# A third chain, in two halves of tiles, for a layer's second feed-forward in a two-layer fused kernel

## The reference, cut to what matters

```python
h = layernorm(x) * ln1_g + ln1_b
src2 = diff_attn(h) @ Wo.T + bo          # 16 x 16 heads inside a row, rmsnorm of each head's output
conn = x + src2
h2 = layernorm(conn) * ln2_g + ln2_b
y = conn + relu(h2 @ W1.T + b1) @ W2.T + b2   # 256 -> 1024 -> 256
x = x + y
x = x + product_key_ffn(layernorm(x))    # sim = n5 @ cmat (1024 scores a row), top 16 of 64 twice,
                                         # top 16 of their 50 sums, softmax, gelu(n5 @ wd50) @ wu50
```

## Time and profile before

| | us |
|---|---|
| median of 3 runs (lowest, highest) | 3261.49 (3259.35, 3266.36) |
| the profiled execution's own time | 3247.05 |
| its span, first to last instruction | 3245.3 |
| first group's front alone | 0 to 290 |
| seven joint groups | 290 to 2934, 376 to 379 each |
| last group's back alone | 2934 to 3245.3 |

### The profile page before, as it was taken

The page is one execution under the profiler, slowest core; times in us unless marked ns, Lnnn a source line. Parts: engine busy times, 40 slices in busy tenths (PEclk is TensorE's granted clock), DMA queues, the critical chain, the costliest instruction groups (busy, mean ns, idle before and its releaser), DMA issues. The chain is left out here.

```text
span 3245.3 us, 47685 instructions
## 1 busy us (share of the span) xinstructions
PE 2507.4 (77%) x16384; PEld 1810.7 (56%) x16384; DVE 1848.2 (57%) x7166; ACT 879.3 (27%) x1914; POOL 875.3 (27%) x1076
## 2 busy tenths in 40 slices
PE   5796898768885889848987699858999489876544
PEld 3585567545763558635675457635586356753422
DVE  2313456755648548574557556485485645673557
ACT  1212242223422233222421234222332224212210
POOL 0002114222233223241143223332232411432042
PEclk8698999979997999979998789978999699986666
DMA  6085145141533326241451416333261314512100
GB/s 234 13 281 200 66 127 205 65 148 40 194 137 112 140 78 225 76 141 64 134 197 66 148 46 203 120 125 127 81 227 70 139 66 128 203 66 108 27 0 7
DMA packets 215066, 392.39 MB, mean 121 GB/s; under 512 B 83728, under 2 KB 167952, under 8 KB 189616
## 3 DMA queue, kind: packets, MB, share of 16 engines
...
HBM read 350.55 MB, written 38.67 MB: 120 GB/s over the span
## 5 line engine op out<-in xcount | busy, mean ns | idle before, releaser
L869 PE MATMUL ps<-xbT,stream 128*128 128x128 f32 x2560 | 316.8, 278 | 11.1 <-DMA stream<-in_experts 6.6
L869 PEld LDWEIGHTS ps<-xbT,stream 128*128 128x128 f32 x2560 | 303.4, 193 | 29.6 <-DMA stream<-in_experts 14.4
L301 POOL TENSOR_TENSOR hTB<-pb,sbuf 128x2048 f32<-128x2048 f32 x32 | 152.3, 4772 | 394.8 <-DVE pb L1829 394.8
L529 POOL TENSOR_TENSOR rstdB<-veB,mhalf 128x3 f32<-128x3 f32 (+1 forms) x112 | 81.2, 725 | 589.3 <-DVE veB L1433 562.4
L481 POOL TENSOR_TENSOR rstdA<-veA,mhalf 128x4 f32<-128x4 f32 x24 | 24.5, 1019 | 634.0 <-DVE veA L1404 634.0
L882 PE MATMUL ps<-stream,hTA 128*128 128x256 f32 x640 | 152.5, 381 | 18.0 <-DVE hTA L1662 12.2
L1112 PE MATMUL ps<-ident,work 128*50 128x128 f32 x32 | 12.0, 375 | 194.9 <-POOL work L643 194.9
L869 PE MATMUL ps<-xbT,ctxA 128*128 128x128 f32 x1280 | 157.8, 277 | 2.5 <-DMA ctxA<-in_experts 2.5
L869 PEld LDWEIGHTS ps<-xbT,ctxA 128*128 128x128 f32 x1280 | 150.8, 192 | 12.0 <-DMA ctxA<-in_experts 6.5
L680 PE MATMUL ps<-cmat,aTB 128*128 128x512 f32 x256 | 123.6, 628 | 20.9 <-DVE sbuf L1918 10.7
L1766 DVE TENSOR_TENSOR xB<-ps,xB 128x256 f32<-128x256 f32 x32 | 13.6, 425 | 218.2 <-PE ps L1007 217.3
...
## 6 DMA issues: line engine op xcount, KB each, us to landing
...
```

The costliest lines, as they stand in the source:

```text
L301: return e.tensor_tensor(out.rearrange("p (a d h) -> p a d h", a=8, d=16), a.unsqueeze(2).broadcast_to([P, 8, 16, 16]), vals[:, t, :].rear ...
L529: nc.gpsimd.tensor_tensor(rstdB[:, span(tag, p)], veB[:, span(tag, p)], mhalf[:, 0:len(PARTS[tag][p])], ALU.pow).then_inc(pool_done, O.ste ...
L869: ins = mm(ps[:, 2 * (b % 2) + u, f * P:(f + 1) * P], wu[:, u, k, f * P:(f + 1) * P], xbT[:, b % 2, k, :], start=k == 0, stop=k == KT - 1)
```

## The change

1. ORDER gets a third letter, "s", for a **side** chain. It takes the norm `h2`, the feed-forward, the norm `n5` and the product `h50` with `wd50` out of the back chain (15 slots fewer: 103) and does them in two halves of two tiles: 10 slots for each half and one for `h50`. The new ORDER has 192 letters.
2. A half has its own PSUM bank (6 for half 0, 7 for half 1) and its own 2048 columns for the ReLU's output (`hF2`, in `work`). An `f1` product is now 256 columns wide, its two outputs share the bank's halves, and each pair of outputs waits for the ReLU of the pair before.
3. In the new ORDER half 0 starts behind value slot 3.c and ends ahead of selection slot 0.0: `h2` around block 9, `f1` and `f2` with block 10 and value slots 4.a to 5.c between them, then the gate of 11. Half 1's norm `h2` comes just ahead of selection 0.0, its `f1` between selection 0.0 and 0.2 with the up product of 11, its `f2` and `n5` behind selection 1.1, with the up product of 12, then `h50`. The up product of block 14 again stands between selection 2.1 and 2.2; as many instructions of VectorE follow it as before.
4. `l4 o` moves from VectorE to GpSimd, right behind the power, and works in place in `ob`; the values' sums go to `ob` in SBUF and no longer to PSUM bank 6; `prod` has one buffer, `rep64` moves to `hTB`.
5. The relay has a semaphore for each tile: the write of tile 1 is issued ahead of the read of tile 0, those of 2 and 3 around the read of tile 1, and the expert blocks' row loads come behind all of them.
6. ORDER also changes earlier: some front slots of the first 40 stand one or two places elsewhere, the third slot of the shared expert's end stands ahead of `v`, and the first gate product stands behind two score slots, no longer ahead of them.

```diff
 ORDER = (
-    "bbbfbbbfbbfbfbfbfbffbfbffbfbfbffbfbfbbfbbffbfbffbffbfbbfbfbffbfbbbbfbffbfbbbbffbbffbbbffbbfbbffb"
-    "fbbfffbbfbffbbffbfbfbbfbbfbbbbbbbbbbbbbbbbbbbfbfbbbbbfbbbfbfbfbfffbfbbbbbbbbbbbbbbbbfbbbbb"
+    "bbbfbbfbbfbfbbfbfbfbfbbfffbffbfbfbfbfbfbbffbfbffbffbfbbfbfbffbfbbbfbbbffbbfbbbffbbffbfbfbbbbbfbf"
+    "ffbfbfbffbbbffbfbfsfsbfbsfssbbssbssbfsssbsbsfssbbbbfbbsssfssbbfbbbffbfffbbbfbbbbbbbbbbbbbbbfbbbb"
 )
...
-        prod = work[:, 0:4096].rearrange("p (s n) -> p s n", s=2)
+        prod = work[:, 0:2048]
...
-        raw = ps[:, 6, :].rearrange("p (s n) -> p s n", s=2)
+        hF2 = work[:, 2048:4096].rearrange("p (f n) -> p f n", f=FF // P)
...
-        rep64 = sbuf[:, 0:1024].rearrange("p (a k) -> p a k", a=NPH)
+        rep64 = hTB[:, 2048:3072].rearrange("p (a k) -> p a k", a=NPH)
...
-        PARTS = dict.fromkeys(("y1", "y2", "h2", "n5"), (range(T - 1), range(T - 1, T)))
-        PARTS.update(dict.fromkeys(("y3", "z", "h1"), (range(HALF), range(HALF, T))))
-
-        TURNED = dict.fromkeys(("y1", "y2", "h1", "h2"), ((5, 0), (6, 0)) * 2)
-        TURNED["n5"] = ((6, 0), (7, 0)) * 2
+        PARTS = dict.fromkeys(("y1", "y2"), (range(T - 1), range(T - 1, T)))
+        PARTS.update(dict.fromkeys(("y3", "z", "h1", "h2", "n5"), (range(HALF), range(HALF, T))))
+
+        TURNED = dict.fromkeys(("y1", "y2", "h1"), ((5, 0), (6, 0)) * 2)
...
-                        def relay(t):
+                        def relay_out(t):
                             sp.wait_ge(act_done, A["qk", t])
                             sp.dma_start(qk[:, t * P:(t + 1) * P, :].rearrange("c n d -> n c d"),
-                                         qk_rows[:, t, :].rearrange("p (c d) -> p c d", c=2)).then_inc(qk_out, 16)
-                            sp.wait_ge(qk_out, 16 * (t + 1))
+                                         qk_rows[:, t, :].rearrange("p (c d) -> p c d", c=2)).then_inc(qk_out[t], 16)
+
+                        def relay_in(t):
+                            sp.wait_ge(qk_out[t], 16)
                             for c, cols, landed in ((1, k_cols, k_in[t]), (0, sbuf[:, 0:1024], q_in)):
                                 sp.dma_start(cols[:, t * D:(t + 1) * D].rearrange("p (n a) -> p n a", n=8),
                                              qk[c, t * P:(t + 1) * P, :].rearrange("(n i) (d a) -> (i d) n a", i=16, d=8)).then_inc(landed, 16)
                         yield
-                        for t in range(T):
-                            relay(t)
-                            yield
-                        for _ in range(9 + 2 + (T + 2) * 3 + 1 + 8 + T + 1 + 1):
+                        relay_out(0)
+                        relay_out(1)
+                        yield
+                        relay_in(0)
+                        yield
+                        relay_out(2)
+                        relay_in(1)
+                        relay_out(3)
+                        yield
+                        relay_in(2)
+                        relay_in(3)
...
+                                pool.wait_ge(pool_done, O["rms", i - 1])
+                                o3 = ob[:, i - 1, :].rearrange("p (a d) -> p a d", a=16)
+                                nc.gpsimd.tensor_tensor(o3, o3, b16(mx[:, (i - 1) % 2, 0:16], 16), ALU.mult).then_inc(
+                                    pool_done, O.step("l4", "o", i - 1))
...
+                    def side():
+                        for p in range(2):
+                            rstd("h2", p)
+                            yield
+                            for t in PARTS["h2"][p]:
+                                wait_scaled(pool, "h2", t)
+                                add("cb", t, xnB[:, t], xnB[:, t], w["b2a"])
+                            for t in PARTS["h2"][p]:
+                                pool.wait_ge(pool_done, O["cb", t])
+                                add("xc", t, xB[:, t], xB[:, t], xnB[:, t])
+                            yield
+                            for _ in range(4 + 2):
+                                yield
+                            rstd("n5", p)
+                            yield
+                            yield
...
+                    def side():
+                        for p in range(2):
+                            bank, tt, cols = 6 + p, PARTS["h2"][p], slice(p * 2 * P, (p + 1) * 2 * P)
+                            yield
+                            for t in tt:
+                                turn("h2", t, hh, TURNED["h2"][t])
+                            yield
+                            for f in range(FF // P):
+                                if f == 0:
+                                    pe.wait_ge(act_done, A["h2", "T", tt[1]])
+                                elif f % 2 == 0:
+                                    pe.wait_ge(act_done, A["h2", "relu", p, f - 1])
+                                for k in range(KT):
+                                    ins = mm(ps[:, bank, f % 2 * 2 * P:(f % 2 + 1) * 2 * P], kt("w1a")[:, k, f * P:(f + 1) * P],
+                                             aTB[:, k, cols], start=k == 0, stop=k == KT - 1)
+                                ins.then_inc(pe_done, PE.step("h2", "f1", p, f))
+                                if f % 2:
+                                    yield
+                            w2v = w["w2a"].rearrange("p (f d) -> p f d", f=FF // P)
+                            pe.wait_ge(act_done, A["h2", "relu", p, FF // P - 1])
+                            for t in tt:
+                                for f in range(FF // P):
+                                    ins = mm(ps[:, bank, t % 2 * D:(t % 2 + 1) * D], hF2[:, f, t % 2 * P:(t % 2 + 1) * P], w2v[:, f, :],
+                                             start=f == 0, stop=f == FF // P - 1)
+                                ins.then_inc(pe_done, PE.step("h2", "f2", t))
+                                yield
+                            yield
+                            for t in tt:
+                                turn("n5", t, xnB, TURNED["n5"][t])
+                            yield
+                        pe.wait_ge(act_done, A["n5", "T", T - 1])
+                        for t in range(T):
+                            ins = project(ps[:, 7, t * NP:(t + 1) * NP], aTB, t, kt("wd50"), slice(0, NP))
+                        ins.then_inc(pe_done, PE.step("h50"))
+                        yield
+
...
+                    def side():
+                        for p in range(2):
+                            yield
+                            turned("h2", p, ("v", T - 1), ("lg2", "lb2"))
+                            yield
+                            for f in range(FF // P):
+                                if f % 2 == 0:
+                                    act.wait_ge(pe_done, PE["h2", "f1", p, f + 1])
+                                sa(hF2[:, f, :], ps[:, 6 + p, f % 2 * 2 * P:(f % 2 + 1) * 2 * P], ACT.Relu, bias=w["b1a"][:, f:f + 1]).then_inc(
+                                    act_done, A.step("h2", "relu", p, f))
+                                if f % 2:
+                                    yield
+                            yield
+                            yield
+                            yield
...
-                            if i >= 2:
-                                t = i - 2
-                                v.wait_ge(pool_done, O["rms", t])
-                                v.wait_ge(vec_done, V["pred", t, 1])
-                                vv.tensor_tensor(ob[:, t, :].rearrange("p (a d) -> p a d", a=16),
-                                                 raw[:, t % 2, :].rearrange("p (a d) -> p a d", a=16),
-                                                 b16(mx[:, t % 2, 0:16], 16), ALU.mult).then_inc(vec_done, V.step("l4", "o", t))
...
+                    def side():
+                        for p in range(2):
+                            variance("h2", p)
+                            yield
+                            scaled_part("h2", p, xnB, hh)
+                            yield
+                            for _ in range(4 + 2):
+                                yield
+                            for t in PARTS["n5"][p]:
+                                v.wait_ge(pe_done, PE["h2", "f2", PARTS["n5"][p][-1]])
+                                v.wait_ge(pool_done, O["xc", t])
+                                vv.tensor_tensor(xB[:, t, :], ps[:, 6 + p, t % 2 * D:(t % 2 + 1) * D], xB[:, t, :], ALU.add).then_inc(
+                                    vec_done, V.step("h2", "f2", t))
+                                stats("n5", xB, smallB, t)
+                            variance("n5", p)
+                            yield
+                            scaled_part("n5", p, xB, xnB)
+                            yield
...
-            group(g, "fb")
-        group(G, "b")
+            group(g, "fbs")
+        group(G, "bs")
```

120 lines of the change are left out of this document (38 added, 82 removed).

## The result

The changed kernel takes 3243.3 us in the median (3236.5 to 3247.6); beside it, in the same rounds, the kernel before took 3261.5 us (3249.3 to 3266.4). The ratio is 0.9952, with a 95% interval of 0.9934 to 0.9970: 10 to 22 us faster. On a second chip it was 0.9959 (0.9940 to 0.9978). The forecast was 3216.5 us, 45 us faster. The direction was right and the time lies in the stated range, but the gain was forecast two and a half times too large.

The account below looks back on a forecast made before the run. No single engine: a joint group was TensorE's work up to block 14, then VectorE's tail. Seven joint groups at -4.3 (-30) and -15 for the last took 3247.05 to 3202, median forecast 3216.5 us, range 3168 to 3264.

Parts of the forecast that it names:

- the earlier edits of ORDER (first 40 slots): Front of each group: slots swap places with the same work, no sure wait gained or lost; 0, bounds -1.5 and +1.5.
- The tail "keeps its length": Joint group from `hid` of block 14 to the selection's end, nearly all VectorE's own work: stays 38.2 us.
- `hid` 14: VectorE's `hid` of block 14 started 2.7 us after its up product; it would now wait for the product: -2.7 us.
- Relay and start of the scores: Joint group: earlier relay write lets the scores start sooner and `combine` end earlier; -1.6 us, bounds 0 and -3.0.
- `f1` in half widths: Joint group's feed-forward: 64 records of 256 columns take 14.0 us against 17.4; -3.0 us, bounds -3.4 and 0.
- old and new waits: TensorE from `combine` to block 14: old waits of 8.9 us go, new ones of 11.9 come, bounds 8.9 and 16.
- Slower: Rival: TensorE's in-order queue held at the ReLU waits; at 1.3 us longer each, +64, 3326 us; chance 0.11.
- nothing: Rival: new waits are 16 us and the clock falls in a half; within 0.2%, 3266 us; chance 0.09.
- better filling: Rival: new waits stay at or below 8.9 us and front slots gain; -76 to -104, about 3170 us; chance 0.24.
- `l4 o` on GpSimd: Joint group's value stage: moving this multiply off VectorE costs nothing, 0; if its cover is gone, 2.9 us a group.
- The last group: Without expert blocks the side chain truly overlaps: relay -4.0, earlier selection -11.3; -15 us, bounds -20 and -4.
- the rival of a low clock through all of half 0: Last group: half 0's products take 13.4 us more and eat the 11.3 gained; 3228 us; chance 0.14.

Follow-up runs that it names:

- e3: The kernel before with only the first 30 letters of ORDER taken from the changed kernel: 3270.3 us, ratio 1.0060 to the kernel before.
- e1: The changed kernel with the first 30 letters of ORDER as in the kernel before: 3224.0 us, ratio 0.9922 to the kernel before.
- e14: e1 run again beside the changed kernel on one chip: 21 us faster than the changed kernel in these rounds.
- e4: The kernel before with only the new relay, ORDER unchanged: 3244.9 us, ratio 0.9982 to the kernel before.
- e6: The changed kernel with the first 30 letters of ORDER as before and the relay in series again: 3229.0 us, ratio 0.9925 to the kernel before.
- e7: e1 with the output scaling `l4 o` back on VectorE, in place in SBUF: 3331.9 us, ratio 1.0232 to the kernel before.
- e13: The changed kernel run again, unedited, on the same chip as e14: 21 us slower than the old front in these rounds.
- e5: The changed kernel with only the first 14 letters of ORDER as before: 3240.7 us, ratio 0.9943 to the kernel before.
- e9: The changed kernel with layer 0's output projection done twice for tiles 2 and 3: 3234.4 us, ratio 0.9954 to the kernel before.

## Why the prediction was right and wrong, point by point

**The step that failed: "the earlier edits of ORDER (first 40 slots) exchange slots with the same work: 0", bounds -1.5 and +1.5 for a group.** It measured +3.6 us up to `f2` in the joint groups of the changed kernel, +3.8 in e3. Undone alone it gave back 10 to 21 us. The waits hardly differ, as the idle times under e1 and e3 show; what went is the granted clock, 0.82 to 0.68 over these 30 us. Not all of the 3.6 is this: with the old front and the old clock e1 and e14 are still 1.7 and 1.8 late. So the first 30 letters account for about 2 us of it; the rest is in part the 0.7 that e4 shows between executions and in part the letters behind them. The forecast doubted the clock around the halves and in the last group, never in the front.

**The tail "keeps its length".** This step failed too: it grew from 38.2 to 40.1 us, 1.9 in a group and 13 in all. The premise, `hid` 14 at the same place of the selection, was right. That VectorE had no waits there before because it was late was overlooked, though the earlier trace rows show `hid` 14 without a wait.

**Relay and start of the scores, -1.6.** -1.8 was measured, so the number came out right by luck: the write is indeed issued some 6 us earlier (6.2 in e4), but the scores of the joint groups don't wait for it, and the relay alone gives nothing there (e4, e6).

**`f1` in half widths, old and new waits, `hid` 14: -2.7 together.** -3.3 was measured, but its parts are not those forecast. Means over seven groups: `hid` 14 starts 0.1 us behind its up product and no longer 2.7, as forecast. The waits grew from 9.0 to 10.2 us, by 1.2 and not 3.0. `f1` went from 16.0 to 15.4 us: a gain of 0.5 where 3.0 was forecast, since a record of 256 columns took 0.24 us there and not the 0.22 of `f2`. The other 1.6 us less are TensorE's time for its other products. The misses on `f1` and on the waits cancel. In joint group 4 TensorE waits 12 times, for 10.2 us, from behind `combine` to block 14, against the 11.9 forecast. Its timeline has the kinds that the forecast named:

```profile
1645.80 1.96 PE L904 MATMUL ps<-stream,hTA 128*128 128x256 f32 x8 [1.07 <-issue]
...
1663.03 1.13 PE L712 MATMUL ps<-wo,oTB 128*128 128x256 f32 x4 [1.32 <-ACT oTB L1222]
...
1690.92 1.99 PE L1140 MATMUL ps<-aTB,w1a 128*128 128x256 f32 x8 [0.93 <-ACT work L1417]
...
1697.89 2.42 PE L1149 MATMUL ps<-w2a,work 128*128 128x256 f32 x10 [0.93 <-ACT work L1417]
...
1710.38 0.76 PE L697 MATMUL ps<-ident,sbuf 128*128 128x128 f32 x4 [1.06 <-DVE sbuf L1488]
...
1755.49 3.73 PE L891 MATMUL ps<-xbT,stream 128*128 128x128 f32 x32
```

The down product of block 3 waits 1.07 us (forecast 1.0), each of four pairs 0.93 (1.1, though a ReLU of 256 columns took 0.47 us and not 0.42), norm `h2` of half 1 1.06 (1.3), and the output products 3.3 together instead of 2.1. Half 1's `n5` and `h50` were to cost 1.7 us and cost one wait of 0.73. "Slower", by ReLU waits 0.5 us longer each, and "nothing", with waits of 16, did not come. Neither did "better filling": the waits stayed above 8.9. Of the forecast's signs of being right, `hid` 14 behind its up product and the early MAX8 (counted from the group's start) came; the period of 370 to 375 us (it is 378) and the tail of 38 didn't.

**`l4 o` on GpSimd, 0.** In the changed kernel it is 0.62 us an operation, and in the joint groups no engine waits for it, so the term stood. The other place isn't cheap any more: with the sum in SBUF, VectorE pays 4.7 us and not 0.4 for about half of the tiles (e7).

**The last group, -15.** -12.6 was measured in this execution and -8.2 in e13, the same kernel; the two differ ahead of the scores, which start at 114.1 and 118.6 us of the group (119.3 before). The relay is worth 4.5 of it by e4 (forecast 4.0). Its landmarks on VectorE and TensorE:

```profile
3121.12 0.42 DVE L1922 TENSOR_TENSOR xnB<-ps,xnB 128x256 f32<-128x256 f32 x1 [1.76 <-PE ps L712]
...
3161.62 2.20 DVE L1935 MAX8 sbuf<-ps 128x8 f32<-128x64 f32 x16 [5.50 <-PE ps L702]
...
3195.76 2.20 DVE L1935 MAX8 sbuf<-ps 128x8 f32<-128x64 f32 x16 [0.59 <-PE ps L702]
```

```profile
3054.59 7.11 PE L1069 MATMUL ps<-work,sbuf 32*32 32x128 f32 x160 [6.69 <-ACT work L1357]
...
3126.97 3.78 PE L1140 MATMUL ps<-aTB,w1a 128*128 128x256 f32 x8 [1.66 <-ACT aTB L1189]
3131.68 3.78 PE L1140 MATMUL ps<-aTB,w1a 128*128 128x256 f32 x8 [0.93 <-ACT work L1417]
3136.39 1.99 PE L1140 MATMUL ps<-aTB,w1a 128*128 128x256 f32 x8 [0.93 <-ACT work L1417]
```

Counted from the group's start (2940.5 after, 2931.8 before) the first MAX8 comes 21.5 us earlier, and tile 2's 12.7; the earlier trace rows have those of before. The first scores' wait is 6.7 us instead of 10.1. The low clock was there for two pairs of half 0 (3.78 us each) and gone for the third, one pair more than I took: 1.9 us of the missing 2.4. So the rival of a low clock through all of half 0 did not come.

**The sum.** Forecast -4.3 a joint group; measured +0.4 in the trace: +3.6 in the front, where the clock fell, and +1.9 in the tail, both forecast as 0, against -5.1 in the stretches between, forecast as -4.3. By the medians, 18.2 us in all with 8.2 to 12.6 of them in the last group, a joint group gained 0.8 to 1.4. With the old front the whole is 25 to 38 us, against the forecast's 45.

**Open.** Single joint groups of one kernel differ by 2 to 5 us from group to group and from execution to execution, and the clock goes with it. A mean over seven groups of one execution is thus no better than 1 us or so. The trace of e5 is 3 us slower than that of the kernel before from joint group 1 on, and e5 is 0.9943 of it by its runs: it was profiled 10 us above its median, the kernel before 14.4 below. (The joint groups of that trace take 375.4 to 380.8 us, a little more apart than the 376 to 379 given above.) The changed front costs 21 us in one comparison and 10 in the other; each is uncertain by about 10 us, so they don't contradict each other, and the true price isn't settled. Nor is it shown why the level falls earlier with the changed front: that its work is thinner there is inferred from e9's answer to more work, and TensorE's busy time over 70 to 100 us is 25.7 us before and 25.5 after in the mean.
